# First FFN product of the first token block moved into the weight preparation of a gated-recurrence and FFN kernel

## Chip, cores and metric

The kernel runs on all 8 cores of one Trainium2 chip. Each core works on two of the 16 sequences and prepares all weights for itself. The metric is the device time in microseconds of the slowest core; a comparison takes the median of several runs.

## The reference, cut to what matters

```python
def attn(x, W_r, W_i, lambd):
    r = sigmoid(einsum('btd,ed->bte', x, W_r))
    i = sigmoid(einsum('btd,ed->bte', x, W_i))
    log_a = 8.0 * r * log_sigmoid(lambd)
    a = exp(log_a)
    b = sqrt(maximum(1.0 - exp(2.0 * log_a), 0.0)) * (i * x)
    return scan(h[t] = a[t] * h[t-1] + b[t])

def absmean(W):                       # ternary weights
    gamma = mean(abs(W)) + 1e-6
    return sign(W / gamma) * minimum(round(abs(W / gamma)), 1.0)

def ffn(x, W_fc, ln_w, ln_b, W_proj):
    h = gelu(einsum('btd,hd->bth', x, absmean(W_fc)))
    h = layernorm(h, ln_w, ln_b)
    return einsum('bth,dh->btd', h, absmean(W_proj))

x = x + attn(layernorm(x), W_r, W_i, lambd)
x = x + ffn(layernorm(x), W_fc, ln_w, ln_b, W_proj)
```

x is 16 sequences of 2048 tokens with D = 1024 channels, the hidden width H is 4096. Quantizing a weight needs the mean of its absolute values, so each weight is read twice: once for the sum, once to be compared with the threshold.

## The kernel before

A core takes its two sequences in eight blocks of T = 512 tokens (index k), channels on the partitions. A block's x is 8 tiles of 128 x 512 in `xb0` or `xb1`, by turns. For each k: layer norm 1 (`emit_ln1`), gates and scan (loop over e, lines 606 to 710), statistics of layer norm 2, its normalized tiles (`emit_ln2_tile_one`, six on VectorE and two on GpSimd), the first FFN product with Gelu (lines 761 to 792), and the second one (`emit_y_group`, spread over the gates of the next block). Block k = 0 also carries the preparation of the weights:

- Lines 210 to 226 convert W_r and W_i.
- During the gates of k = 0, `emit_gfc_loads` and `emit_gfc_abs` (L247, L257) read W_fc once and sum its absolute values.
- `emit_prep2a_mid` (lines 290 to 343) reads W_fc a second time in 32 pieces of 128 x 1024 (512 KB, L304) into four slots of `xb1`. VectorE quantizes each in two instructions (L319, L323) into `wfc_q`, which stays in SBUF. Beside it W_proj is read for the first time in 32 pieces (L314) into four slots made of the scratch tiles t_a, t_q, t_b, t_i, and ScalarE sums its absolute values (L331, activation Abs). After every second piece up to i = 14 one tile of layer norm 2 is emitted. The threshold of W_proj follows (`emit_thr`, L263).
- The FFN loop of k = 0 (lines 761 to 792): for each of 32 column blocks h, TensorE does 8 products (L767), ScalarE the Gelu (L775), GpSimd the square (L782; for k > 0 VectorE does it), and TensorE adds value and square into the statistics of layer norm 3, two blocks late (L753, L755, `emit_ln3_stat`). In the same loop W_proj is prepared piece by piece: `emit_prep2b_load` (L353) three pieces ahead, `emit_prep2b_piece` (VectorE L364 and L367, two small products L373 and L375), and `emit_prep2b_fold` two pieces late (VectorE L386, then a store to the DRAM buffer `wp_sc` by `emit_scatter`, L205).

The order of work is written by hand. Each engine runs its own list of instructions strictly in the order in which `emit` appended them, and a wait holds up all that stands behind it on that engine. DMAs are issued from such lists too: pieces in even slots from SyncE, those in odd slots from GpSimd. L304 and L314 of one slot count on one semaphore, and `emit` makes each DMA wait for the one before it on the same semaphore:

```python
            if inc.startswith("d_") and self.semc[inc] > 0:
                self.wait(eng, (inc, self.semc[inc]))
```

For an odd i GpSimd's list therefore has: wait until the slot is quantized (VectorE), issue L304, wait for its landing, issue L314.

Of the kernel before, what the change touches and what calls it, by code (L numbers as in the profile page):

```python
# [64 lines left out]
def build_nc(nsup=NSUP, debug=False):  # L65
# [221 lines left out]
        setfree(key, tln2)  # L287
        return tln2

    def emit_prep2a_mid(xb, tok_bc2, tok_i7, tok_gbl):  # L290
        nonlocal tok_wfc, tok_thrp
        ln2_toks = {}
        b.wait("tensor", gfc_state["last"])
        b.wait("tensor", tok_ones)
        tok_thrf = emit_thr(accf, 0, 0)
        red_p = None
        for i in range(32):
            pc, kd = i // 8, i % 8
# [26 lines left out]
            setfree(("qn4", sl), tq)
            setfree(("stg", sl), tq)
            if kd == 7:
                tok_wfc_pc[pc] = tq
            b.wait("scalar", tl2)
            red_p = b.emit("scalar", lambda E, st2=st2, i=i:  # L330
                           E.activation(st2, st2, AF.Abs, accum_out=accp[:, i:i + 1]), inc="s")  # L331
            setfree(("tstg", sl), red_p)
            if i % 2 == 0 and i // 2 < ND:
                ln2_toks[i // 2] = emit_ln2_tile_one(i // 2, xb, tok_bc2, tok_i7, tok_gbl)
        tok_wfc = tok_wfc_pc[3]
        b.wait("tensor", red_p)
        tok_thrp = emit_thr(accp, 1, 3)
        for sl in range(4):
            usewait("sync", ("stg", sl))
        dst1 = xping[1][:, :].rearrange("p (c t) -> p c t", c=ND)  # L340
        src1 = Xd[0, :, T:2 * T].rearrange("(c p) t -> p c t", p=128)
        tok_x[1] = b.emit("sync", lambda E, d=dst1, s=src1: E.dma_start(d, s), inc="d_x1", n=16)
        return (ln2_toks[5], ln2_toks[7])
# [252 lines left out]
    for k in range(nsup):  # L596
# [113 lines left out]
                emit_ln2_stat_chunk(k, xb, e - 1)  # L710

        tstat2 = emit_ln2_stat_chunk(k, xb, ND - 1)
        tok_bc2 = rows_and_bcast(tstat2, 2, rs_t, mb_t, prev_read=tok_ln1, prev_read_g=tok_ln1g)
        if k == 0:
            tok_ln2 = emit_prep2a_mid(xb, tok_bc2, tok_ri[(k, ND - 1)][1], tok_gb_last)
        else:
            lt = [emit_ln2_tile_one(c, xb, tok_bc2, tok_ri[(k, ND - 1)][1], tok_gb_last)
                  for c in range(ND)]
# [15 lines left out]
                src2 = Xd[sq2, :, t02:t02 + T].rearrange("(c p) t -> p c t", p=128)  # L734
                tok_x[kk] = b.emit("sync", lambda E, d=dst2, s=src2: E.dma_start(d, s), inc=f"d_x{kk % 2}", n=16)

        b.wait("tensor", tok_ln2[0])
        b.wait("tensor", tok_ln2[1])
        if k > 0:
            b.wait("tensor", tok_wfc)  # L740
        else:
            for i3 in range(3):
                emit_prep2b_load(i3)
        gs_toks = {}

        def emit_ln3_stat(h):
            tge2, tgs2 = gs_toks[h]
            b.wait("tensor", tge2)
            b.wait("tensor", tgs2)
            if h == 0:  # L750
                usewait("tensor", ("pS",))
                usewait("tensor", ("pQ",))
            b.emit("tensor", lambda E, h=h: E.matmul(pS[:, :], ones_bf[:, :], gch(h),  # L753
                                                     start=(h == 0), stop=(h == NH - 1)))
            tq = b.emit("tensor", lambda E, h=h: E.matmul(pQ[:, :], ones_bf[:, :],  # L755
                                                          gsq[:, (h % 3) * T:(h % 3 + 1) * T],
                                                          start=(h == 0), stop=(h == NH - 1)), inc="pe")
            setfree(("gsq", h % 3), tq)
            return tq

        for h in range(NH):
            bank = h % 4
            if k == 0:
                b.wait("tensor", tok_wfc_pc[h // 8])
            usewait("tensor", ("pool", bank))
            for d in range(ND):
                fn = lambda E, h=h, d=d, bank=bank: E.matmul(  # L767
                    pool[bank][:, :], wfc_q[:, d * H + h * 128: d * H + h * 128 + 128], lnch(d),
                    start=(d == 0), stop=(d == ND - 1))
                if d == ND - 1:  # L770
                    tu = b.emit("tensor", fn, inc="pe")
                else:
                    b.emit("tensor", fn)
            b.wait("scalar", tu)
            tge = b.emit("scalar", lambda E, h=h, bank=bank: E.activation(  # L775
                gch(h), pool[bank][:, :], AF.Gelu), inc="s")
            setfree(("pool", bank), tge)
            tok_gelu[(k, h)] = tge
            geng, ginc = ("gpsimd", "g") if k == 0 else ("vector", "v")
            b.wait(geng, tge)  # L780
            usewait(geng, ("gsq", h % 3))
            tgs = b.emit(geng, lambda E, h=h: E.tensor_tensor(  # L782
                gsq[:, (h % 3) * T:(h % 3 + 1) * T], gch(h), gch(h), ALU.mult), inc=ginc)
            gs_toks[h] = (tge, tgs)
            if k == 0:
                if h + 3 < NH:
                    emit_prep2b_load(h + 3)
                emit_prep2b_piece(h)
                if h >= 2:
                    emit_prep2b_fold(h - 2)  # L790
            if h >= 2:
                tq3 = emit_ln3_stat(h - 2)
        tq3 = emit_ln3_stat(NH - 2)
        tq3 = emit_ln3_stat(NH - 1)
        prev_rs3 = tok_yev.get((k - 1, ND - 1)) if k >= 1 else None
        if k == 0:
            emit_prep2b_tail()
# [96 lines left out]
```

How the kernel before makes its waits and increments, by code:

```python
    def emit(self, eng, fn, inc=None, n=1):  # L41
        if inc is not None:
            if inc.startswith("d_") and self.semc[inc] > 0:
                self.wait(eng, (inc, self.semc[inc]))
            self.semc[inc] += n
            tok = self.semc[inc]
            h = self.semh[inc]
            self.prog[eng].append(lambda E, fn=fn, h=h, n=n: fn(E).then_inc(h, n))
            return (inc, tok)
        self.prog[eng].append(fn)
        return None
# [1 line left out]
    def wait(self, eng, tok):  # L53
        if tok is None:
            return
        name, v = tok
        assert v <= self.semc[name], f"wait on future token {name}={v}"
        if self.maxw[eng].get(name, 0) >= v:
            return
        self.maxw[eng][name] = v
        h = self.semh[name]
        self.prog[eng].append(lambda E, h=h, v=v: E.wait_ge(h, v))
```

## Time and profile before

| | us |
|---|---|
| median of 3 runs (2371.64 to 2518.87) | 2372.93 |
| the profiled execution | 2364.18 |
| its span, slowest core | 2362.6 |
| spans of its eight cores | 2355.1 to 2362.6 |

The profiled execution is one run under the hardware profiler. The span goes from the first to the last instruction of a core; 1.6 us of the execution's time lie around it. The whole weight preparation lies in the first 502 us of it; the other seven token blocks take the rest. Engines are named PE (TensorE), DVE (VectorE), ACT (ScalarE), POOL (GpSimd) and SP (SyncE); PEld are the weight loads of TensorE. DMA-issuing instructions of GpSimd are listed with their engine but not counted as busy.

### The profile page before, as it was taken

To read this page: it belongs to the slowest core of one execution; us is meant where nothing else is said; L and a number is where in the kernel's file an instruction comes from. 1 tells how busy PE (TensorE), PEld (TensorE's weight loads), DVE (VectorE), ACT (ScalarE), POOL (GpSimd) and SP (SyncE) were. 2 spreads that over 40 slices of the span, in tenths; PEclk is the share of its full clock that TensorE was granted. 3 is DMA by queue.
4 is the path that set the end of the run, shared out by engine and by line. 5 is a ranking of instruction groups with operands and counts; after the bars stand their busy time and mean duration, and the time that the engine had idled before them with its cause. 6 is when DMAs were issued, how large, how long until landed. Compare 5 with 4: busy or idle time off the path is not lost.

```text
span 2362.6 us, 20089 instructions; the slowest of 8 cores (2355.1 to 2362.6 us)
## 1 busy us (share of the span) xinstructions
PE 1503.0 (64%) x6052; PEld 613.5 (26%) x6052; DVE 987.8 (42%) x1505; ACT 619.4 (26%) x1013; POOL 275.2 (12%) x260
## 2 busy tenths in 40 slices
PE   0333005755849685886769584958496767868597
PEld 0011001221314232332224131413142323323243
DVE  1423755645451444335442544244524443254413
ACT  0165221112322132223322232223221332223220
POOL 1211213421010101001010101010101001010100
PEclk9766557986969798888979796979798888979798
DMA  7564786751302130212121131123021212112103
GB/s 187 144 189 147 226 257 206 187 130 62 116 26 73 45 116 27 98 45 82 61 98 45 43 101 60 39 71 106 10 98 45 91 53 98 45 62 81 63 27 125
DMA packets 103746, 223.68 MB, mean 95 GB/s; under 512 B 34516, under 2 KB 34516, under 8 KB 103640
## 3 DMA queue, kind: packets, MB, share of 16 engines
q1 hardware_dynamic: 91352, 178.34, 23.6%
q0 software_dynamic: 12288, 44.05, 6.7%
q8 instruction: 52, 0.85, 0.1%
q14 instruction: 54, 0.44, 0.1%
HBM read 192.98 MB, written 29.37 MB: 94 GB/s over the span
## 4 chain that ended last, share of the span: by engine, by line
PE 44%; DVE 21%; ACT 12%; DMA 9%; issue 9%; POOL 3%; DVEq 1%; ACTq 0%; POOLq 0%; SPq 0%
PE pool L767 18%; PE pY L485 9%; PE pool L616 6%; DMA xb<-wfct 4%; DVE t_b L698 3%; POOL t_b L693 3%; PE pS L753 2%; PE pQ L755 2%; DVE tmp L586 2%; DVE ln_bf L588 2%; DVE tmp L284 2%; DVE ln_bf L286 2%; PE pS L459 2%; ACT t_a L657 2%; DVE t_q L682 2%
## 5 line engine op out<-in xcount | busy, mean ns | idle before, releaser
L767 PE MATMUL pool<-ln_bf,wfc_q 128*128 128x512 bf16 x2048 | 502.4, 391 | 99.6 <-DVE ln_bf L286 99.6
L485 PE MATMUL pY<-g_sb,wp_sl 128*128 128x512 bf16 x2048 | 472.6, 392 | 65.5 <-DVE tmp L507 47.3
L767 PEld LDWEIGHTS pool<-ln_bf,wfc_q 128*128 128x128 bf16 x2048 | 205.1, 101 | 367.7 <-issue 140.9
L485 PEld LDWEIGHTS pY<-g_sb,wp_sl 128*128 128x128 bf16 x2048 | 204.9, 100 | 326.7 <-issue 99.8
L775 ACT ACTIVATE g_sb<-pool 128x512 bf16<-128x512 f32 x256 | 152.9, 597 | 436.4 <-PE pool L767 436.3
L782 DVE TENSOR_TENSOR gsq<-g_sb 128x512 bf16<-128x512 bf16 x224 | 95.4, 426 | 389.3 <-ACT g_sb L775 377.0
L616 PE MATMUL pool<-ln_bf,wr_sl 128*128 128x512 bf16 x512 | 160.0, 469 | 114.3 <-DVE ln_bf L588 114.3
L651 ACT ACTIVATE t_r<-pool 128x512 f32<-128x512 f32 x64 | 38.1, 595 | 508.8 <-PE pool L616 508.8
L565 PE MATMUL pS<-xbr,ones_bf 128*128 128x512 bf16 x64 | 30.4, 475 | 211.6 <-DVE sqr L559 211.6
L693 POOL TENSOR_TENSOR t_b<-t_q,ln_bf 128x512 f32<-128x512 f32 x64 | 73.8, 1153 | 772.7 <-ACT t_q L687 772.7
L674 DVE SCALAR_TENSOR_TENSOR t_q<-t_a 128x512 f32<-128x512 f32 x64 | 44.3, 692 | 270.4 <-ACT t_a L662 270.4
L627 PE MATMUL pool<-ln_bf,wi_sl 128*128 128x512 bf16 x512 | 123.1, 384 | 0.0
L616 PEld LDWEIGHTS pool<-ln_bf,wr_sl 128*128 128x128 bf16 x512 | 59.6, 118 | 215.8 <-issue 180.3
L586 POOL TENSOR_TENSOR t_r<-xb,rs_t 128x512 f32<-128x512 f32 x16 | 25.6, 1598 | 759.7 <-DVE mb_t L469 758.5
L698 DVE TENSOR_TENSOR_SCAN t_b<-t_a,carry,t_b 128x512 f32<-128x512 f32 x48 | 61.6, 1284 | 104.8 <-POOL t_b L693 104.8
L753 PE MATMUL pS<-g_sb,ones_bf 128*128 128x512 bf16 x256 | 98.0, 383 | 4.0 <-DVE gsq L782 4.0
L755 PE MATMUL pQ<-gsq,ones_bf 128*128 128x512 bf16 x256 | 97.8, 382 | 0.0
L436 PE MATMUL pS<-xbr,ones_bf 128*128 128x512 bf16 x64 | 31.3, 490 | 103.8 <-DVE sqr L430 103.5
L459 PE MATMUL pS<-rows,ones_kf 1*128 1x512 f32 x48 | 41.6, 961 | 87.4 <-DVE rows L457 87.4
L446 ACT ACTIVATE rows<-pS,cst 1x512 f32<-1x512 f32 x24 | 16.3, 677 | 297.2 <-PE pQ L438 231.8
L263 PE MATMUL pool<-accp,ones_f 128*128 128x32 f32 x2 | 0.6, 396 | 127.2 <-ACT t_i L331 127.2
L682 DVE SCALAR_TENSOR_TENSOR t_q<-t_q,t_i 128x512 f32<-128x512 f32 x64 | 44.3, 692 | 64.5 <-ACT t_q L678 64.5
(118 smaller groups left out, 1667.0 us busy)
## 6 DMA issues: line engine op xcount, KB each, us to landing
wp_sl<-wp_sc SPq DMA_DIRECT2D x128, 512.0 KB, 3.9
xb<-x SPq DMA_DIRECT2D x8, 2048.0 KB, 9.6
wr_sl<-wr_sc SPq DMA_DIRECT2D x64, 256.0 KB, 3.1
wi_sl<-wi_sc SPq DMA_DIRECT2D x64, 256.0 KB, 2.9
xb<-wfct SPq DMA_DIRECT2D x32, 512.0 KB, 5.7
xb<-wfct POOLq DMA_DIRECT2D x32, 512.0 KB, 5.9
y<-xb SPq DMA_DIRECT2D x8, 2048.0 KB, 7.8
t_a<-wpt SPq DMA_DIRECT2D x16, 512.0 KB, 5.7
```

The lines of the kernel that those rows point to most:

```text
L459: tb1 = b.emit("tensor", lambda E: E.matmul(pS[:, :], ones_kf[:, :], s2, start=True, stop=True), inc="pe")
L485: fn = lambda E, kh=kh, sl=sl, bank=bank, first=(kh == 0), last=last: E.matmul(pY[bank][:, :], wp_sl[:, sl * 2048 + (kh % 16) * 128: sl * ...
L616: fn = lambda E, d=d, sl=sl, pR=pR: E.matmul(pR[:, :], wr_sl[:, sl * D + d * 128: sl * D + d * 128 + 128], lnch(d), start=(d == 0), stop=( ...
L627: fn = lambda E, d=d, sl=sl, pI=pI: E.matmul(pI[:, :], wi_sl[:, sl * D + d * 128: sl * D + d * 128 + 128], lnch(d), start=(d == 0), stop=( ...
L682: tvm = b.emit("vector", lambda E, q=q: E.scalar_tensor_tensor(t_q[:, q * T:(q + 1) * T], t_q[:, q * T:(q + 1) * T], 0.5, t_i[:, q * T:(q ...
L693: tgb = b.emit("gpsimd", lambda E, q=q, e=e: E.tensor_tensor(t_b[:, q * T:(q + 1) * T], t_q[:, q * T:(q + 1) * T], lnch(e), ALU.mult), inc ...
L698: tA = b.emit("vector", lambda E, q=q, init=init: E.tensor_tensor_scan(t_b[:, q * T:(q + 1) * T], t_a[:, q * T:(q + 1) * T], t_b[:, q * T: ...
L753: b.emit("tensor", lambda E, h=h: E.matmul(pS[:, :], ones_bf[:, :], gch(h), start=(h == 0), stop=(h == NH - 1)))
L755: tq = b.emit("tensor", lambda E, h=h: E.matmul(pQ[:, :], ones_bf[:, :], gsq[:, (h % 3) * T:(h % 3 + 1) * T], start=(h == 0), stop=(h == N ...
L767: fn = lambda E, h=h, d=d, bank=bank: E.matmul(pool[bank][:, :], wfc_q[:, d * H + h * 128: d * H + h * 128 + 128], lnch(d), start=(d == 0) ...
L775: tge = b.emit("scalar", lambda E, h=h, bank=bank: E.activation(gch(h), pool[bank][:, :], AF.Gelu), inc="s")
L782: tgs = b.emit(geng, lambda E, h=h: E.tensor_tensor(gsq[:, (h % 3) * T:(h % 3 + 1) * T], gch(h), gch(h), ALU.mult), inc=ginc)
```

## The change

24 of the 32 column blocks of the first FFN product of k = 0, with their Gelus, squares and statistics, move from the W_proj loop into the loop of `emit_prep2a_mid`: block i-8 is emitted at the end of iteration i, for i = 8 to 31. So that their input is there, the eight tiles of layer norm 2 are emitted in iterations 0 to 7, one each, where they were emitted in iterations 0, 2, ... 14. Blocks 24 to 31 stay in the W_proj loop, beside its first eight pieces, and its other 24 pieces have none beside them. For k > 0 nothing changes. The body of the FFN loop becomes the function `emit_ffn_h`; its square is on GpSimd for k = 0 as before. Lines move: the square is L758 after, the Gelu L751, the block's products L742.

```diff
@@ emit_prep2a_mid, end of the loop over i @@
-            if i % 2 == 0 and i // 2 < ND:
-                ln2_toks[i // 2] = emit_ln2_tile_one(i // 2, xb, tok_bc2, tok_i7, tok_gbl)
+            if i < ND:
+                ln2_toks[i] = emit_ln2_tile_one(i, xb, tok_bc2, tok_i7, tok_gbl)
+            if i >= 8:
+                emit_ffn_h(i - 8, ln2wait=(ln2_toks[5], ln2_toks[7]) if i == 8 else None)
@@ main loop, before the normalization of layer norm 2 @@
+        def emit_ffn_h(h, ln2wait=None):
+            bank = h % 4
+            if ln2wait is not None:
+                b.wait("tensor", ln2wait[0])
+                b.wait("tensor", ln2wait[1])
+            if k == 0:
+                b.wait("tensor", tok_wfc_pc[h // 8])
+            usewait("tensor", ("pool", bank))
...
+            b.wait("scalar", tu)
+            tge = b.emit("scalar", lambda E, h=h, bank=bank: E.activation(
+                gch(h), pool[bank][:, :], AF.Gelu), inc="s")
...
+            geng, ginc = ("gpsimd", "g") if k == 0 else ("vector", "v")
+            b.wait(geng, tge)
+            usewait(geng, ("gsq", h % 3))
+            tgs = b.emit(geng, lambda E, h=h: E.tensor_tensor(
+                gsq[:, (h % 3) * T:(h % 3 + 1) * T], gch(h), gch(h), ALU.mult), inc=ginc)
+            gs_toks[h] = (tge, tgs)
+            if h >= 2:
+                emit_ln3_stat(h - 2)
@@ main loop, in place of the loop over h @@
+            for j in range(8):
+                emit_ffn_h(24 + j)
+                emit_prep2b_load(j + 3)
+                emit_prep2b_piece(j)
+                if j >= 2:
+                    emit_prep2b_fold(j - 2)
+            for j in range(8, NH):
+                if j + 3 < NH:
+                    emit_prep2b_load(j + 3)
+                emit_prep2b_piece(j)
+                emit_prep2b_fold(j - 2)
```

GpSimd's list before, in the middle of `emit_prep2a_mid` (iterations 17, 19, 21 and 23): a load of W_fc into `xb`, a load of W_proj into t_q or t_i, and so on.

```order
L304 DMA xb<-wfct 128x1024 [waits v,d_stg1]
L314 DMA t_q<-wpt 128x1024 [waits s,d_stg1]
L304 DMA xb<-wfct 128x1024 [waits v,d_stg3]
L314 DMA t_i<-wpt 128x1024 [waits s,d_stg3]
L304 DMA xb<-wfct 128x1024 [waits v,d_stg1]
L314 DMA t_q<-wpt 128x1024 [waits s,d_stg1]
L304 DMA xb<-wfct 128x1024 [waits v,d_stg3]
L314 DMA t_i<-wpt 128x1024 [waits s,d_stg3]
```

The same place of GpSimd's list after the change:

```order
L304 DMA xb<-wfct 128x1024 [waits v,d_stg1]
L314 DMA t_q<-wpt 128x1024 [waits d_stg1]
L758 TENSOR_TENSOR gsq<-g_sb 128x512 [waits s,pe] x2
L304 DMA xb<-wfct 128x1024 [waits v,d_stg3]
L314 DMA t_i<-wpt 128x1024 [waits d_stg3]
L758 TENSOR_TENSOR gsq<-g_sb 128x512 [waits s,pe] x2
```

Two squares of `gsq`, each waiting for ScalarE (s) and TensorE (pe), now stand between the load of W_proj of one pair and the load of W_fc of the next.

ScalarE's list before, at the end of `emit_prep2a_mid` (the Abs of W_proj pieces, then all Gelus of k = 0):

```order
L331 ACTIVATE t_a,accp<-t_a 128x1024 [waits d_stg0]
L331 ACTIVATE t_q,accp<-t_q 128x1024 [waits d_stg1]
L331 ACTIVATE t_b,accp<-t_b 128x1024 [waits d_stg2]
L331 ACTIVATE t_i,accp<-t_i 128x1024 [waits d_stg3]
L775 ACTIVATE g_sb<-pool 128x512 [waits pe] x32
```

The same place after the change:

```order
L331 ACTIVATE t_a,accp<-t_a 128x1024 [waits d_stg0]
L751 ACTIVATE g_sb<-pool 128x512 [waits pe]
L331 ACTIVATE t_q,accp<-t_q 128x1024 [waits d_stg1]
L751 ACTIVATE g_sb<-pool 128x512 [waits pe]
L331 ACTIVATE t_b,accp<-t_b 128x1024 [waits d_stg2]
L751 ACTIVATE g_sb<-pool 128x512 [waits pe]
L331 ACTIVATE t_i,accp<-t_i 128x1024 [waits d_stg3]
L751 ACTIVATE g_sb<-pool 128x512 [waits pe] x9
```

A Gelu stands behind each Abs, and the last nine Gelus (blocks 23 to 31) follow the last Abs.

## Rows read from the trace of the kernel before

**Rows 1.** Busy time by stretches: start:end, length, engines, then PEclk, DMA share, GB/s

```profile
235.00:366.00 131.00, 3.78 (x9) 1.65 (x8) 77.84 (x82) 34.24 (x62) 22.85 (x34) 0.50 0.78 238
366.00:502.00 136.00, 99.31 (x385) 33.59 (x383) 90.62 (x102) 20.78 (x34) 61.55 (x62) 0.90 0.70 189
```

**Rows 2.** Waits from 235 to 366 us: us in total, times, longest

```profile
PE pool L263 <- ACT t_i L331: 127.2, 1, 127.2
```

**Rows 3.** Chain of waits from 220 to 580 us: start, us, what

```profile
289.59 7.86 DMA xb<-wfct
298.56 7.28 DMA xb<-wfct
```

**Rows 4.** Timeline of one pair: start, us, engine, line, tile, [idle before, releaser]

```profile
298.00 0.53 POOL L314 DMA_DIRECT2D t_i<-wpt  x1 [7.69 <-DMA xb<-wfct]
298.56 0.53 POOL L304 DMA_DIRECT2D xb<-wfct  x1
...
303.38 1.06 ACT L331 ACTIVATE t_i<-t_i 128x1024 f32<-128x1024 f32 x1 [8.59 <-DMA t_i<-wpt]
...
304.43 1.04 ACT L331 ACTIVATE t_a<-t_a 128x1024 f32<-128x1024 f32 x1
...
305.94 0.75 DVE L319 TENSOR_SCALAR qn_buf<-xb,thr 128x1024 bf16<-128x1024 f32 x1 [4.19 <-DMA xb<-wfct]
306.38 0.53 POOL L314 DMA_DIRECT2D t_q<-wpt  x1 [7.29 <-DMA xb<-wfct]
```

**Rows 5.** Timeline of GpSimd, first and last pair counted, and a layer norm tile

```profile
250.71 0.56 POOL L314 DMA_DIRECT2D t_q<-wpt  x1 [4.58 <-DVE wfc_q L323]
...
260.62 0.53 POOL L304 DMA_DIRECT2D xb<-wfct  x1
...
275.98 1.27 POOL L284 TENSOR_TENSOR t_r<-xb,rs_t 128x512 f32<-128x512 f32 x1
...
279.42 0.72 POOL L304 DMA_DIRECT2D xb<-wfct  x1
...
352.92 0.53 POOL L304 DMA_DIRECT2D xb<-wfct  x1
```

**Rows 6.** Timeline of TensorE, ScalarE and GpSimd: a block, table load, Gelu, square

```profile
365.92 3.19 PE L767 MATMUL pool<-ln_bf,wfc_q 128*128 128x512 bf16 x8
...
369.19 1.28 ACT L775 ACT_TABLE_LOAD   x1 [3.84 <-PE pool L767]
...
408.15 0.60 ACT L775 ACTIVATE g_sb<-pool 128x512 bf16<-128x512 f32 x1 [2.19 <-PE pool L767]
...
408.96 1.03 POOL L782 TENSOR_TENSOR gsq<-g_sb 128x512 bf16<-128x512 bf16 x1 [1.21 <-ACT g_sb L775]
```

**Rows 7.** The W_fc loads of L247, 82 to 198 us: issue to landing

```profile
DMA to landing us min/median/max: 4.0/5.2/7.8
```

**Rows 8.** Timeline of VectorE and GpSimd: piece 8, a steady pair, the end

```profile
402.13 0.82 DVE L364 TENSOR_SCALAR qn_buf<-t_a,thr 128x1024 bf16<-128x1024 f32 x1
...
469.17 1.26 DVE L386 TENSOR_SCALAR qn_buf<-qn_buf,lnw_pp 128x1024 bf16<-128x1024 bf16 x1
...
471.07 0.97 POOL L205 DMA_DIRECT2D wp_sc<-qn_buf  x1 [0.91 <-DVE qn_buf L386]
...
474.72 0.75 DVE L364 TENSOR_SCALAR qn_buf<-t_q,thr 128x1024 bf16<-128x1024 f32 x1 [1.83 <-DMA wp_sc<-qn_buf]
...
476.78 1.26 DVE L386 TENSOR_SCALAR qn_buf<-qn_buf,lnw_pp 128x1024 bf16<-128x1024 bf16 x1
...
501.26 0.67 DVE L404 COPY tmp<-pY 2x512 f32<-2x512 f32 x1
```

**Rows 9.** Waits of VectorE from 402 to 502 us

```profile
DVE qn_buf L364 <- DMA wp_sc<-qn_buf: 28.4, 12, 5.3
```

**Rows 10.** The folds of L386, 366 to 502 us: ns min/median/max

```profile
L386 DVE TENSOR_SCALAR qn_buf<-qn_buf,lnw_pp x32: 475/482/1265, 379.7 to 500.9; 128x1024 bf16<-128x1024 bf16 x32
```

**Rows 11.** Timeline of ScalarE: an Exp (L455) and the first Abs behind it

```profile
232.32 0.72 ACT L455 ACTIVATE rows<-rows,cst 1x512 f32<-1x512 f32 x1
232.95 1.04 ACT L331 ACTIVATE t_a<-t_a 128x1024 f32<-128x1024 f32 x1
```

More of the change, by code:

```diff
@@ L288, in emit_ln2_tile_one, with emit_prep2a_mid @@
         return tln2
-    def emit_prep2a_mid(xb, tok_bc2, tok_i7, tok_gbl):
+    def emit_prep2a_mid(xb, tok_bc2, tok_i7, tok_gbl, emit_ffn_h):
         nonlocal tok_wfc, tok_thrp
@@ L712, in build_nc, with emit_ln3_stat @@
         tstat2 = emit_ln2_stat_chunk(k, xb, ND - 1)
+        gs_toks = {}
+        ffn_state = {"tu": None}
+        def emit_ln3_stat(h):
+            tge2, tgs2 = gs_toks[h]
+            b.wait("tensor", tge2)
+            b.wait("tensor", tgs2)
+            if h == 0:
+                usewait("tensor", ("pS",))
+                usewait("tensor", ("pQ",))
+            b.emit("tensor", lambda E, h=h: E.matmul(pS[:, :], ones_bf[:, :], gch(h),
+                                                     start=(h == 0), stop=(h == NH - 1)))
+            tq = b.emit("tensor", lambda E, h=h: E.matmul(pQ[:, :], ones_bf[:, :],
+                                                          gsq[:, (h % 3) * T:(h % 3 + 1) * T],
+                                                          start=(h == 0), stop=(h == NH - 1)), inc="pe")
+            setfree(("gsq", h % 3), tq)
+            return tq
@@ new lines, in emit_ffn_h @@
+        def emit_ffn_h(h, ln2wait=None):
[6 more added lines that the diff above has]
+            usewait("tensor", ("pool", bank))
+            for d in range(ND):
+                fn = lambda E, h=h, d=d, bank=bank: E.matmul(
+                    pool[bank][:, :], wfc_q[:, d * H + h * 128: d * H + h * 128 + 128], lnch(d),
+                    start=(d == 0), stop=(d == ND - 1))
+                if d == ND - 1:
+                    tu = b.emit("tensor", fn, inc="pe")
+                else:
+                    b.emit("tensor", fn)
+            ffn_state["tu"] = tu
+            b.wait("scalar", tu)
+            tge = b.emit("scalar", lambda E, h=h, bank=bank: E.activation(
+                gch(h), pool[bank][:, :], AF.Gelu), inc="s")
+            setfree(("pool", bank), tge)
+            tok_gelu[(k, h)] = tge
+            geng, ginc = ("gpsimd", "g") if k == 0 else ("vector", "v")
[6 more added lines that the diff above has]
+                emit_ln3_stat(h - 2)
@@ L713, in build_nc @@
         tok_bc2 = rows_and_bcast(tstat2, 2, rs_t, mb_t, prev_read=tok_ln1, prev_read_g=tok_ln1g)
         if k == 0:
-            tok_ln2 = emit_prep2a_mid(xb, tok_bc2, tok_ri[(k, ND - 1)][1], tok_gb_last)
+            tok_ln2 = emit_prep2a_mid(xb, tok_bc2, tok_ri[(k, ND - 1)][1], tok_gb_last, emit_ffn_h)
         else:
@@ L735, in build_nc @@
                 tok_x[kk] = b.emit("sync", lambda E, d=dst2, s=src2: E.dma_start(d, s), inc=f"d_x{kk % 2}", n=16)
-        b.wait("tensor", tok_ln2[0])
-        b.wait("tensor", tok_ln2[1])
         if k > 0:
+            b.wait("tensor", tok_ln2[0])
+            b.wait("tensor", tok_ln2[1])
             b.wait("tensor", tok_wfc)
+            for h in range(NH):
+                emit_ffn_h(h)
         else:
@@ L743, in build_nc @@
                 emit_prep2b_load(i3)
[L744 to L792, printed above, removed]
@@ L793, in build_nc @@
+            for j in range(8):
[9 more added lines that the diff above has]
+                emit_prep2b_fold(j - 2)
         tq3 = emit_ln3_stat(NH - 2)
         tq3 = emit_ln3_stat(NH - 1)
+        tu = ffn_state["tu"]
```

## Prediction

> **What bounds the kernel now.** I read the busy time by stretches first, then the chain of waits, then the timeline of one pair of iterations, then the waits of the stage behind. The stretches [rows 1] split the preparation in two: 131 us in which TensorE is busy 3.78 us at the low level of its clock (granted 0.50, 1.2 of 2.4 GHz) while the DMA engines are busy 0.78 of the time (W_fc quantized, W_proj summed: call it stage A), and 136 us in which TensorE is busy 99 us at 0.90 (W_proj quantized, with the first FFN product beside it: stage B). In stage A the only large waiter is the threshold product of TensorE, 127.2 us for the last Abs [rows 2]. So TensorE has room for FFN work there, and the question is whether that work can be put in without slowing what paces the stage.
>
> What paces it is one queue. The chain of waits names the same piece again and again, a W_fc load issued by GpSimd [rows 3]. The timeline of one pair says why [rows 4]: L314 for an odd i is issued at 298.00, L304 for the next odd i right behind it at 298.56, and then GpSimd stands until that load has landed (ScalarE's Abs for the first starts at 303.38, VectorE takes the second at 305.94, GpSimd goes on at 306.38). The two loads of a slot share a semaphore, and each issue waits for the one before on it, so the queue has two loads in flight and turns once per landing. From the L304 of i=9 at 260.62 to that of i=31 at 352.92 are 11 pairs [rows 5]: 92.3 us, 8.39 each.
>
> **The change, part by part.** (1) 24 of the 32 FFN column blocks move into stage A, one per iteration from i=8. On TensorE that is free: a block took 3.27 us there at the low level (365.92 to the table load that waited for it at 369.19) [rows 6]; the two statistics products of a block, as wide as one of its eight each, are then a quarter of that, 0.8. Two blocks with theirs are 8.2 us per pair, below the period that follows. On ScalarE two Gelus of 0.60 us per pair are small too.
>
> (2) The squares L782 (L758 after) are on GpSimd, and there they stand between the DMA issues. After the change GpSimd's row per pair is L304, L314, square, square. The first square waits for Gelu(i-8), and on ScalarE that stands behind Abs(i), which waits for the L314 load that GpSimd has just issued. The second stands behind Abs(i+1) and Gelu(i-7). Only then comes the next L304. Nothing of this queue is in flight meanwhile; SyncE runs ahead but VectorE takes the slots in order and so is paced by GpSimd too. The new period is the sum of what lies in series:
> - L304 issued until its data are in: T. The trace has 7.38 us (298.56 to 305.94), but behind another load of the same queue; L314, which is first in its queue, has 5.38 (298.00 to 303.38) with three more loads in flight [rows 4]. The shortest landing of a W_fc load in the earlier stage is 4.0 us [rows 7]. After the change each load is alone in its queue, with about one of SyncE beside it; I take the middle of 4.0 and 5.4: 4.7.
> - GpSimd goes on 0.44 us after VectorE does (305.94, 306.38) [rows 4]: 0.45.
> - L314 until Abs(i): T again, 4.7.
> - Abs(i) to Gelu(i-8) 1.05 (303.38 to 304.43 is Abs to the next on ScalarE [rows 4]), Gelu 0.60, Abs(i+1) 1.05, Gelu start to square start 0.81 and the square 1.03 (408.15, 408.96) [rows 6]: 4.54. Its data are there, since SyncE is ahead.
> Sum 9.4 + 0.45 + 4.54 = 14.4 us in place of 8.39. Over 11 pairs: 158.4 against 92.3, +66.1. With T = 4.0 for both it is 13.0 and +50.6; with today's 7.38 and 5.38, 17.8 and +103.
>
> (3) The second layer norm's tiles are all in the first eight iterations. VectorE's have no price of their own: GpSimd's path is later. GpSimd's two tiles go from i=12 and 14 to 6 and 7, 3.44 us each (275.98 to the next issue at 279.42) [rows 5]. From L314 of i=5 at 250.71: tile 6 until 254.7, L304 of i=7, which lands about 261 (6 us, since SyncE's queue is full here), L314 at 261.5, tile 7 until 265.5, then FFN block 0, 3.3 (268.8), table load 1.3, Gelu to square 0.81 and square 1.03: about 272.2 for the L304 of i=9, before at 260.62 [rows 5, 6]. +11.6.
>
> (4) What follows the last load is as before: the 2 MB load of x and the first W_proj loads start off VectorE's last quantization. 0.
>
> (5) Stage B. Its first eight pieces still have a block each (24 to 31): nothing. The other 24 took from 402.13 to 501.26, 99.1 us or 8.26 per pair [rows 8]. VectorE is short of nothing but the store of two pieces ahead: it waited 28.4 us, 12 times, each for a store to wp_sc [rows 9], and all of them for GpSimd's. The steady pair: fold ends 470.43, store issued 471.07, buffer free 474.72 (4.29), piece 2.06, fold 1.26 [rows 8] = 7.6. The fold takes 0.482 at the median and 1.265 at the longest [rows 10], the long ones beside work on GpSimd. With no square beside it, I count 0.48: 0.78 by 12 pairs = 9.4 gained; if the rest above 7.6 (0.66 a pair) goes as well, 17. I take -13. Bounds: 0, if stores and loads are the limit; -38, if VectorE alone sets the pace (24 by 2.54 = 61).
>
> For the fold the Trainium skill (SBUF — State Buffer, section SBUF: two separate sides) has a rule: VectorE in a two-port mode and GpSimd share one port pair, the second to come waits for the whole instruction, and descriptors that GpSimd writes for its own DMAs wait too. The long folds agree with it. By the rule alone every long fold goes with the squares, which is the -9.4, and GpSimd's store issue, which stays, may keep some; the sum is the same within that.
>
> Sum: 66.1 + 11.6 - 13 = +64.7 on the profiled execution's 2364.2 us: 2428.9. The median of the runs shown is 2372.9, 8.7 above it, so 2438 for the median after.
>
> **Rivals.**
> - The work fits in the gaps (other side). If the squares stall GpSimd only while it would have waited for its load anyway, stage A keeps 8.39 per pair and only stage B changes: -13, at best -38, so 2335 to 2360. For it: GpSimd stands idle 6 to 8 us of each pair today. Against: that idle time is the landing of a load in flight, and the new waits come when none is. The point from which it decides: with the 11.6 us of the start and -13 behind, nothing is lost up to 8.5 us a pair, and with the whole -38 up to 10.8; the series has 5.0 us before any load, so both landings together would have to take under 3.5 or under 5.8. 0.06.
> - Loads quicken and stage B gains much. T = 4.0 and -30: 50.6 + 11.6 - 30 = +32, 2405, within 2%. For it: stage A moved 238 GB/s [rows 1] and would move some 150; stage B has 28 us of waits to lose. 0.15.
> - Loads stay as slow as now, T of 5.4 for both: 15.8 per pair, +81 + 12 - 10 = +83, 2456. It is inside my case.
> - Table loads. Abs and Gelu now alternate on ScalarE. If each switch loads a table as at 369.19 (1.28 us) [rows 6], four more per pair lie on the series: 5.1 by 11 = 56 more, 2494. Against: Abs follows Exp at 232.95 with no load between [rows 11], so Abs needs none of its own there. 0.06.
>
> The Trainium skill (ScalarE: Activation LUTs, section Table sets: the hidden batching unit) says to batch calls by table set, which speaks against alternating; but it also says that cheap functions, abs among them, are in every set. By its first sentence this rival's time, by the second none of it. The rows above bear the second out for the Exp set; for Gelu's no row here does, hence 0.06.
>
> **How the numbers follow.** My case, series of waits with T of 4.0 to 5.4 and a stage B gain of 5 to 20, gives +45 to +92 and gets 0.73; the rivals 0.06, 0.15 and 0.06. A measurement tells about 2% from no change, 47 us here, so my case is over it save for its lowest edge (0.05). Slower 0.68 + 0.06 = 0.74. Same 0.05 + 0.15 + 0.06 = 0.26, of which 0.02 goes to faster, for both stages beating their bounds: 0.24 and 0.02. Range: 2400 (the second rival's figure, a little below) to 2468 (T of 5.4 with a small gain in stage B); the table case and a full fit are left out.
>
> **What would show it.** Right: GpSimd's L304 issues in stage A some 14 us apart; its squares waiting for Gelu; ScalarE's Abs on GpSimd's loads waiting 8 us or more, those on SyncE's none; DMA share in stage A down from 0.78 to 0.45 or 0.5; threshold product of W_proj near 443; the last 24 pieces of stage B at about 7.2 a pair; one table load for the Gelus. Wrong: a period of 10 us or less, table loads between Abs and Gelu, or stage B shorter by over 25 us.

## The result, and the profile after

| | before | after |
|---|---|---|
| median of the runs, us | 2372.41 (10 runs) | 2433.15 (9 runs) |
| profiled execution, us | 2364.18 | 2429.75 |
| its span, slowest core, us | 2362.6 | 2427.9 |

The ratio of the changed kernel to the one before is 1.0253, 95% interval [1.0239, 1.0267]: slower by 61 us. In some executions of any kernel the cores of one die run at a lower granted clock and the time is some per cent longer: the medians given here include such executions and the ratios leave them out (without them e7, below, has 2354 in place of 2361, e9 2357 in place of 2359), and e4 is read from cores 0 to 3, which were undisturbed.

First the busy time by stretches of the changed kernel (start:end, length, PE, PEld, DVE, ACT, POOL, then TensorE's clock, DMA share, GB/s): stage A, and the 11 pairs inside it alone. GpSimd's DMA issues do count as busy in such rows, otherwise than said ahead: of its 45 instructions in the second row 23 are squares and 22 are issues.

```profile
235.00:435.00 200.00, 77.34 (x238) 28.39 (x242) 77.00 (x82) 46.26 (x85) 45.14 (x56) 0.67 0.49 155
274.00:423.00 149.00, 67.73 (x217) 24.95 (x219) 43.85 (x44) 34.70 (x66) 34.55 (x45) 0.73 0.45 147
```

Against [rows 1] TensorE has found its work in stage A, but the DMA share has fallen from 0.78 to 0.49, and the rate from 238 to 155 GB/s. Nothing more had to be loaded; the loads are only further apart.

One pair of the changed kernel on its timeline (start, length, engine, line, tile, idle before and releaser), the counterpart of [rows 4]:

```profile
302.86 0.59 POOL L304 DMA_DIRECT2D xb<-wfct  x1
...
307.56 0.75 DVE L319 TENSOR_SCALAR qn_buf<-xb,thr 128x1024 bf16<-128x1024 f32 x1 [9.10 <-DMA xb<-wfct]
308.01 0.53 POOL L314 DMA_DIRECT2D t_q<-wpt  x1 [4.56 <-DMA xb<-wfct]
...
311.93 1.06 ACT L331 ACTIVATE t_q<-t_q 128x1024 f32<-128x1024 f32 x1 [10.25 <-DMA t_q<-wpt]
...
312.98 0.58 ACT L751 ACTIVATE g_sb<-pool 128x512 bf16<-128x512 f32 x1
...
313.46 1.04 ACT L331 ACTIVATE t_b<-t_b 128x1024 f32<-128x1024 f32 x1
313.77 1.03 POOL L758 TENSOR_TENSOR gsq<-g_sb 128x512 bf16<-128x512 bf16 x1 [5.23 <-ACT g_sb L751]
314.50 0.58 ACT L751 ACTIVATE g_sb<-pool 128x512 bf16<-128x512 f32 x1
...
315.29 1.04 POOL L758 TENSOR_TENSOR gsq<-g_sb 128x512 bf16<-128x512 bf16 x1 [0.48 <-ACT g_sb L751]
...
316.27 0.59 POOL L304 DMA_DIRECT2D xb<-wfct  x1
```

GpSimd's part of it reads from top to bottom as one series. GpSimd issues a load, waits 4.56 us for it, issues the second, and waits 5.23 us for a Gelu that stands behind the Abs of that second load. Before, the second row of [rows 4] (the next L304) came 0.56 us after L314; now it comes 8.3 us after it. No ACT_TABLE_LOAD stands between Abs and Gelu; the one load is here, ahead of the first Gelu:

```profile
271.60 1.28 ACT L751 ACT_TABLE_LOAD   x1 [2.81 <-PE pool L742]
```

The table gives each kernel of this study by the same marks: the start of GpSimd's L304 of i=9, the mean distance of its L304s from i=9 to i=31, the first quantization of stage B, the time of its first 8 pieces, and of its last 24. Each figure is the median over the cores of one profiled execution, read from each core's timeline.

| kernel | L304 of i=9 | pair | stage B starts | first 8 pieces | last 24 pieces | median, us |
|---|---|---|---|---|---|---|
| before | 258.9 | 8.28 | 369.5 | 29.2 | 99.6 | 2372 |
| after | 273.7 | 13.57 | 442.7 | 30.7 | 88.0 | 2433 |
| e1 squares on VectorE | 262.1 | 7.35 | 365.2 | 29.8 | 88.1 | 2353 |
| e2 squares behind the issue | 263.0 | 8.19 | 374.2 | 30.4 | 88.4 | 2361 |
| e3 tiles only | 262.7 | 7.69 | 367.7 | 29.9 | 100.6 | 2369 |
| e4 wait only | 266.3 | 12.72 | 427.2 | 29.3 | 99.4 | 2429 |
| e5 before, squares on VectorE | 258.5 | 8.25 | 370.7 | 65.8 | 195.9 | 2502 |
| e6 own semaphores | 263.3 | 6.67 | 359.2 | 30.1 | 88.3 | 2345 |
| e7 tiles behind the issue | 260.9 | 7.39 | 365.7 | 30.4 | 88.5 | 2361 |
| e8 contiguous store | 263.8 | 7.27 | 366.3 | 28.5 | 83.1 | 2344 |
| e9 square behind the piece | 259.5 | 8.16 | 370.5 | 27.1 | 88.9 | 2359 |
| e10 as e6, tiles moved | 262.3 | 6.64 | 358.1 | 30.0 | 89.3 | 2344 |
| e11 no block moved | 255.8 | 6.67 | 354.1 | 27.3 | 90.0 | 2339 |
| e12 late squares | 261.9 | 6.68 | 358.2 | 27.5 | 86.0 | 2339 |

For the change itself the first two rows say: +14.8 us up to the L304 of i=9, +58.2 in the 11 pairs (5.29 each), about nothing around stage B's start, +1.5 in its first 8 pieces and -11.6 in the rest.

### The profile page after: what moved, and what is told of

Same layout as the page of the kernel before. It is cut to its first block, busy times and chain, and to the rows that moved or that the text cites. A ratio compares the mean times of both kernels' runs of the same rounds, so it can differ in the third digit from the quotient of the medians.

```text
span 2427.9 us, 19960 instructions; the slowest of 8 cores (2412.8 to 2427.9 us)
## 1 busy us (share of the span) xinstructions
PE 1523.6 (63%) x5932; PEld 619.0 (25%) x6052; DVE 978.7 (40%) x1505; ACT 616.7 (25%) x1013; POOL 271.2 (11%) x260
## 4 chain that ended last, share of the span: by engine, by line
PE 42%; DVE 21%; ACT 13%; issue 10%; DMA 10%; POOL 3%; DVEq 1%; ACTq 0%; POOLq 0%; SPq 0%
PE pool L742 17%; PE pY L487 9%; PE pool L618 6%; DVE t_b L700 3%; POOL t_b L695 3%; DMA xb<-wfct 3%; DMA wp_sc<-qn_buf 3%; PE pQ L727 2%; DVE tmp L588 2%; DVE ln_bf L590 2%; PE pS L725 2%; DVE tmp L284 2%; DVE ln_bf L286 2%; PE pS L461 2%; ACT t_a L659 2%
## 5 line engine op out<-in xcount | busy, mean ns | idle before, releaser
L742 PE MATMUL pool<-ln_bf,wfc_q 128*128 128x512 bf16 x2005 | 514.0, 400 | 146.7 <-DVE ln_bf L286 99.4
L742 PEld LDWEIGHTS pool<-ln_bf,wfc_q 128*128 128x128 bf16 x2048 | 208.0, 102 | 426.6 <-issue 209.9
L758 DVE TENSOR_TENSOR gsq<-g_sb 128x512 bf16<-128x512 bf16 x224 | 95.3, 426 | 389.1 <-ACT g_sb L751 376.9
L751 ACT ACTIVATE g_sb<-pool 128x512 bf16<-128x512 f32 x256 | 152.5, 596 | 362.3 <-PE pool L742 360.0
L319 DVE TENSOR_SCALAR qn_buf<-xb,thr 128x1024 bf16<-128x1024 f32 x32 | 25.0, 781 | 111.8 <-DMA xb<-wfct 111.6
```

What stands on the lines that cost most here:

```text
L742: fn = lambda E, h=h, d=d, bank=bank: E.matmul(pool[bank][:, :], wfc_q[:, d * H + h * 128: d * H + h * 128 + 128], lnch(d), start=(d == 0) ...
L758: tgs = b.emit(geng, lambda E, h=h: E.tensor_tensor(gsq[:, (h % 3) * T:(h % 3 + 1) * T], gch(h), gch(h), ALU.mult), inc=ginc)
```

## The experiments

Each ratio is to executions of the kernel before that were timed together with that experiment. Diffs are cut to the lines that matter; a `...` marks a cut.

**e1, the squares of the moved blocks on VectorE.** GpSimd's list in stage A has only its loads left; TensorE and ScalarE still do the moved blocks.

```diff
-            geng, ginc = ("gpsimd", "g") if k == 0 else ("vector", "v")
+            geng, ginc = ("gpsimd", "g") if k == 0 and h >= 24 else ("vector", "v")
```

> The changed kernel with the squares of blocks 0 to 23 on VectorE, so that GpSimd's list in stage A holds only its loads again. Theory (the squares' waits in GpSimd's list hold up the next load): the period from one L304 of GpSimd to the next over one falls from 13.5 us to 8.4 to 9.0 us, and the time from 2433 to about 2380 (2372 to 2390). Rival (the FFN work itself slows stage A, by sharing SBUF, the DMA engines' memory or ScalarE): the period stays over 12 us and the time over 2420.

Measured: 2353.25 us, ratio 0.9934 [0.9917, 0.9951]; a pair takes 7.35 us. Against the changed kernel that is 80 us less for one line, and it is faster than the kernel before by 0.7%, where 2372 to 2390 had been expected. The expectation missed two things: the pair is shorter than before, of which e3 shows a part (7.69, since no tile stands between the pairs any more), and stage B keeps its gain of 11.5 us. The moved work as such doesn't slow stage A, and the rival falls.

**e2, the squares on GpSimd, but where it waits anyway.** They stand behind the issue of L304 and ahead of L314, where GpSimd waits for its first load.

```diff
+            if i % 2 == 1 and i >= 11:
+                emit_sq(i - 11)
+                emit_sq(i - 10)
...
```

The squares leave `emit_ffn_h` for blocks 0 to 23, and the statistics products follow two blocks later than in the changed kernel.

> The changed kernel with the same squares on the same engine, but two iterations later, between the issues of L304 and L314 of an odd i, where GpSimd waits for a landing anyway; the statistics products follow two blocks later. Theory (the wait at that place, not the work, costs): the period is 8.4 to 9.2 us, GpSimd waits for no Gelu, the time is 2370 to 2385. Rival (the 2.1 us of squares per pair count in full): the period is 10.5 us or more and the time 2395 or more.

Measured: 2361.02 us, ratio 0.9964 [0.9951, 0.9978], 8.19 us a pair, both a little better than expected (2370 to 2385, 8.4 to 9.2). GpSimd's timeline of one pair, with VectorE's quantization of the piece that L304 loads (L314 and L319 are L317 and L322 in this kernel):

```profile
299.22 0.53 POOL L304 DMA_DIRECT2D xb<-wfct  x1
299.76 1.46 POOL L741 TENSOR_TENSOR gsq<-g_sb 128x512 bf16<-128x512 bf16 x1
...
306.64 0.75 DVE L322 TENSOR_SCALAR qn_buf<-xb,thr 128x1024 bf16<-128x1024 f32 x1 [3.48 <-DMA xb<-wfct]
...
307.21 1.08 POOL L741 TENSOR_TENSOR gsq<-g_sb 128x512 bf16<-128x512 bf16 x1 [5.99 <-ACT g_sb L763]
308.24 0.59 POOL L317 DMA_DIRECT2D t_q<-wpt  x1
308.83 0.53 POOL L304 DMA_DIRECT2D xb<-wfct  x1
```

Same engine, same work, 5.4 us less per pair than the changed kernel: the work of the squares was not what cost. The expectation that GpSimd would find every Gelu done was wrong (it waits 5.99 us for the second), but a load of its own is in flight meanwhile. That load is there at 306.64, so only the last 1.2 us or so of wait and square are not covered (306.64 and the 0.44 of GpSimd's delay, to 308.24). Over the pairs it is 8.19 us against e1's 7.35, where GpSimd has no square at all.

**e3, the layer norm tiles alone.** The kernel before, with the change's condition for the tiles and nothing else.

```diff
-            if i % 2 == 0 and i // 2 < ND:
-                ln2_toks[i // 2] = emit_ln2_tile_one(i // 2, xb, tok_bc2, tok_i7, tok_gbl)
+            if i < ND:
+                ln2_toks[i] = emit_ln2_tile_one(i, xb, tok_bc2, tok_i7, tok_gbl)
```

> The kernel before with the eight tiles of layer norm 2 in iterations 0 to 7, no FFN block moved. Theory (of the 14.0 us that the changed kernel loses ahead of the L304 of i=9 the two tiles on GpSimd are a part, the wait for FFN block 0 and its Gelu the rest): that L304 comes 3 to 7 us later than before, and the time rises by 0 to 5 us, since the tiles no longer stand between later loads. Rival (VectorE's six tiles in a row set the start): 10 us or more later.

Measured: 2368.52 us, ratio 0.9994 [0.9976, 1.0011]; the L304 of i=9 comes 3.8 us later, and the pairs behind it take 7.69 us, since the tiles stand between none of them. So 3.8 of the 14.8 us are the tiles. The other 11 are the wait for block 0 and its square: e1 has the tiles and the block but not that wait, and its L304 of i=9 comes at 262.1, as here.

**e4, the wait alone.** The kernel before with one wait more per iteration on GpSimd. No work is added, removed or moved.

```diff
             setfree(("tstg", sl), red_p)
+            if i >= 8:
+                b.wait("gpsimd", red_p)
```

> The kernel before with one wait added per iteration from i=8: GpSimd waits for that iteration's Abs on ScalarE before its next load. Nothing is computed more, less or elsewhere. Theory (a wait behind the landing of L314 puts both landings in series): the period rises from 8.39 to 11.6 us (13.5 less two Gelus of 0.48 and a square of 1.0), over 11 pairs +35 us, time 2400 to 2415. Rival (waiting in GpSimd's list fits in the time in which it waits for landings anyway): the period stays under 9 us and the time within 5 us of before.

Measured: 2429.32 us, ratio 1.0244 [1.0222, 1.0266]. The wait alone costs 58 of the change's 61 us, though the change also gains 11.6 in stage B that this kernel doesn't: in stage A it costs 57.7 us where the change costs 73.2 (stage B starts at 427.2 and 442.7, before at 369.5). It is more than the 30 to 45 expected. The waits of core 2 in the last seven pairs (323 to 406 us; us in total, times, longest):

```profile
POOL xb L304 <- ACT t_a L331: 24.4, 4, 6.3
POOL t_q L314 <- DMA xb<-wfct: 18.4, 4, 5.0
POOL xb L304 <- ACT t_b L331: 18.3, 3, 6.2
POOL t_i L314 <- DMA xb<-wfct: 14.5, 3, 5.0
```

Seven waits of 6.1 us for an Abs and seven of 4.7 for a landing: both landings in series. The L304s of these seven pairs are 11.9 us apart (322.99 to 406.11), close to the 11.6 expected. What the expectation left out are the two tiles at i=12 and 14, which lie in the open in this kernel, and the first wait, which delays the L304 of i=9 by 7.4 us.

**e5, a control that became a finding.** The kernel before with all squares of the first block on VectorE.

```diff
-            geng, ginc = ("gpsimd", "g") if k == 0 else ("vector", "v")
+            geng, ginc = ("vector", "v")
```

> The kernel before with all squares of the first token block on VectorE and no FFN block moved: the control for e1, which was 17 us faster than before. Theory (e1 gains because 24 pieces of stage B have no FFN block and no GpSimd square beside them, and pays nothing in stage A): VectorE gets 0.43 us of square per piece and saves about as much on its folds, so this kernel stays within 5 us of before (2366 to 2376). Rival (e1 gains merely by freeing GpSimd of the squares): about 2353 too.

Measured: 2502.39 us, ratio 1.0559 [1.0528, 1.0589], neither of the two. Stage B takes 262 us in place of 129. VectorE's timeline there:

```profile
423.02 0.42 DVE L782 TENSOR_TENSOR gsq<-g_sb 128x512 bf16<-128x512 bf16 x1 [5.16 <-ACT g_sb L775]
423.36 0.75 DVE L364 TENSOR_SCALAR qn_buf<-t_b,thr 128x1024 bf16<-128x1024 f32 x1
...
430.67 0.43 DVE L782 TENSOR_TENSOR gsq<-g_sb 128x512 bf16<-128x512 bf16 x1 [4.78 <-ACT g_sb L775]
```

The view shows one engine; the rest is read from the lists. The square of block h stands in front of piece h and waits 5 us for its Gelu; on TensorE block h+1 stands behind the products of piece h. So VectorE, TensorE and ScalarE take turns, 7.65 us from one square to the next here.

**e6, more loads in flight.** e1 with semaphores `d_tst0` to `d_tst3` for the W_proj loads, in both stages.

```diff
-                         E.dma_start(st2, WPT[128 * i:128 * (i + 1), :]), inc=f"d_stg{sl}", n=16)
+                         E.dma_start(st2, WPT[128 * i:128 * (i + 1), :]), inc=f"d_tst{sl}", n=16)
...
```

> e1 with semaphores of their own for the W_proj loads, so that L314 no longer waits for the landing of L304 of its slot: up to eight loads are in flight in stage A where there were four. Theory (the period is the landing time that stands in GpSimd's list): GpSimd's period falls from 7.9 us to 7.0 or less and the time from 2353 to 2343 or less. Rival (four loads in flight already take all the bandwidth that the eight cores share, some 265 GB/s each): landings get longer instead, the period stays at 7.6 to 8.0 and the time within 4 us of e1.

Measured: 2345.05 us, ratio 0.9892 [0.9858, 0.9926], 6.67 us a pair. The stretch of its stage A (same columns as above), then the landings there (count, KB each, median us):

```profile
265.00:335.00 70.00, 49.46 (x187) 19.97 (x192) 48.05 (x61) 31.58 (x58) 12.72 (x22) 0.82 0.97 299
```

```profile
xb<-wfct POOLq DMA_DIRECT2D x11, 512.0 KB, 9.0
t_i<-wpt POOLq DMA_DIRECT2D x5, 512.0 KB, 11.6
```

A landing takes 9 to 12 us and still the pair is shorter: with more in flight GpSimd no longer waits for the landing, but ahead of L304, where its list asks for the slot that VectorE frees. From 265 to 335 us five of these waits, 25.8 us, end with VectorE's L323, five more, 27.0 us, the profile puts down to ScalarE, and none to a landing. A DMA share of 0.97 leaves little for still more loads in flight; no run tried them.

**e7, GpSimd's tiles behind the issue.** e1 with the two tiles between L304 and L314 of iterations 5 and 7.

```diff
+            if i in (5, 7):
+                c = 6 + (i - 5) // 2
+                ln2_toks[c] = emit_ln2_tile_one(c, xb, tok_bc2, tok_i7, tok_gbl)
...
-            if i < ND:
+            if i < 6:
```

> e1 with GpSimd's two tiles of layer norm 2 placed between the issues of L304 and L314 of iterations 5 and 7, where it waits for a landing. Theory (a tile in front of an L304 delays it by its 3.4 us, behind it by nothing): the L304 of i=9 comes 2 to 6 us earlier than in e1, and the time falls by 2 to 5 us, to about 2350. Rival (the start is paced by VectorE's quantization, which does not change): the same as e1 within 2 us.

Measured: 2360.74 us, ratio 0.9937 [0.9912, 0.9961], beside e1's 0.9934. The L304 of i=9 came 1.2 us earlier, not 2 to 6: a miss, and the time is the rival's. In place of its tiles GpSimd now waits for VectorE's list ahead of L304: 1.9 to 3.2 us for that of i=7 and 0.3 to 3.2 us for that of i=9, on every core (releaser VectorE L284).

**e8, the store as contiguous rows.** e1 with the pieces stored as rows of 2048 bytes, for the cost of the 256-byte runs of the stores in stage B. It leaves out the right layout: the second product reads its weights in a wrong order.

```diff
-        dst = wp_sc[:, :, i * 128:(i + 1) * 128].transpose([1, 0, 2])
-        src2 = qh.rearrange("p (kd j) -> p kd j", kd=ND)
+        dst = wp_sc.rearrange("k p (q j) -> (k p q) j", j=1024)[128 * i:128 * (i + 1), :]
+        src2 = qh
```

> e1 with every piece of W_proj stored as rows of 2048 bytes in a permuted layout of the same buffer, in place of runs of 256 bytes; the second FFN product then reads its weights in a wrong order (left out: the right layout). Same bytes, an eighth of the packets. Theory (without FFN blocks the pieces of stage B are paced by the cycle fold, store, free buffer, and the 256-byte packets make the store long): stores land in 2.5 to 3 us, VectorE's waits for them mostly go, the last 24 pieces fall from 88 us to 65 to 75, the time to about 2335. Rival (the loads of W_proj, or the memory that all cores share, set the pace): the last 24 pieces stay over 82 us.

Measured: 2343.81 us, two runs, ratio 0.9890 [0.9861, 0.9918]. The store issues of the last 24 pieces (count, KB each, median us to landing), of e1 from 403 to 490 us:

```profile
wp_sc<-qn_buf POOLq DMA_DIRECT2D x12, 256.0 KB, 3.7
...
wp_sc<-qn_buf SPq DMA_DIRECT2D x12, 256.0 KB, 4.0
```

and of e8 from 398 to 482 us:

```profile
wp_sc<-qn_buf SPq DMA_DIRECT2D x13, 256.0 KB, 3.7
wp_sc<-qn_buf POOLq DMA_DIRECT2D x13, 256.0 KB, 2.7
```

The landings are shorter by 0.3 us on one queue and 1.0 on the other, but the pieces take 83.1 us, 5 less than e1, far from 65 to 75 and on the rival's side (over 82). The DMA share falls from 0.76 to 0.67 in these windows. So the 256-byte runs are a small part of stage B; what holds the rest was not separated. The time falls by 9 us against e1, of which about 6 show in stage B; where the rest lies is open.

**e9, e5 with the square one piece later.**

```diff
...
                 emit_prep2b_piece(h)
+                if h >= 1:
+                    emit_sq(h - 1)
+                if h == NH - 1:
+                    emit_sq(h)
```

> e5 (the kernel before with the first block's squares on VectorE, no FFN block moved; it took 2502 us) with each square one piece later in VectorE's list: the square of block h-1 stands behind piece h instead of the square of block h in front of it. Theory (in e5 VectorE waits for Gelu h before piece h, while TensorE's block h+1 stands behind the products of piece h, so the engines work in series, some 8 us per piece where there were 4.2): with the square behind the piece VectorE finds Gelu h-1 done, the 24 last pieces fall from 196 us to 95 to 105 and the time to 2360 to 2385. Rival (VectorE has too little time for squares in stage B): it stays over 2420.

Measured: 2359.19 us, ratio 0.9941 [0.9920, 0.9962]. 143 us come back by the place of one instruction in VectorE's list, slightly more than expected (2360 to 2385; 95 to 105 for the last 24 pieces). More important for the change: the last 24 pieces take 88.9 us with their FFN blocks beside them, and 88.0 in the changed kernel without. The folds there (ns min/median/max):

```profile
L386 DVE TENSOR_SCALAR qn_buf<-qn_buf,lnw_pp x26: 477/479/614, 416.1 to 501.9; 128x1024 bf16<-128x1024 bf16 x26
```

Against [rows 10] the long folds are gone; GpSimd computes nothing here, its 31 instructions from 370 to 502 us are all DMA issues. What stage B gained in the changed kernel can be had by taking the squares off GpSimd, with every FFN block left in place. Whether the short folds or GpSimd's freer list of stores bring it, no run takes apart.

**e10, e6 with both tiles of GpSimd behind its two issues of iteration 7.**

```diff
+            if i == 7:
+                for c in (6, 7):
+                    ln2_toks[c] = emit_ln2_tile_one(c, xb, tok_bc2, tok_i7, tok_gbl)
...
-            if i < ND:
+            if i < 6:
```

> The fastest version so far (e6: squares of blocks 0 to 23 on VectorE, semaphores of their own for the W_proj loads) with GpSimd's two tiles of layer norm 2 both behind the two issues of iteration 7. Theory (in e6 stage A is paced by the DMA engines, 0.95 busy and 314 GB/s, so an issue that comes 3.4 us earlier is served no sooner): within 3 us of e6's 2345, ratio to before 0.987 to 0.991. Rival (the start still waits for GpSimd's issue of iteration 7): 3 to 5 us less than e6.

Measured: 2343.60 us, ratio 0.9899 [0.9865, 0.9933]: as e6.

**e11, no block moved.** e9 with e6's semaphores; the loop of stage A is that of the kernel before.

```diff
-                         E.dma_start(st2, WPT[128 * i:128 * (i + 1), :]), inc=f"d_stg{sl}", n=16)
+                         E.dma_start(st2, WPT[128 * i:128 * (i + 1), :]), inc=f"d_tst{sl}", n=16)
...
                 emit_prep2b_piece(h)
+                if h >= 1:
+                    emit_sq(h - 1)
...
```

> e9 (no FFN block moved, tiles where they were, squares on VectorE behind the piece) with semaphores of their own for the W_proj loads. It asks what moving 24 blocks is worth when nothing stands in GpSimd's list: e6 has both with the blocks moved, 2345. Theory (e9's last 24 pieces take 89 us with the blocks beside them and e1's 88 without, so the blocks cost nothing in stage B and moving them gains nothing): 2343 to 2353. Rival (moving them is worth the 6 us between e1 and e9): 2350 to 2356 or more.

Measured: 2338.57 us, ratio 0.9863 [0.9840, 0.9885], better than either expectation and the fastest with e12.

**e12, all blocks' squares off GpSimd, with the blocks moved.** e6 with the squares of blocks 24 to 31 on VectorE, one piece late.

```diff
             for j in range(8):
                 emit_ffn_h(24 + j)
                 emit_prep2b_load(j + 3)
                 emit_prep2b_piece(j)
+                if j >= 1:
+                    emit_sq(23 + j)
...
+                emit_ln3_stat(22 + j)
+            emit_sq(31)
```

> e6 (blocks moved, own semaphores) with the squares of blocks 24 to 31 on VectorE too, one piece late as in e9, so GpSimd does no square at all. Theory (beside the squares on GpSimd the folds are long and its stores late): the first eight pieces fall from 30 us to 27 to 29 as in e9, the time to about 2343. Rival (in the first eight pieces TensorE's low clock and the landing of x set the pace): no change from e6's 2345 within 2 us.

Measured: 2338.85 us, ratio 0.9868 [0.9848, 0.9889]. The first eight pieces take 27.5 us in place of e6's 30.1, as expected, and the time falls by somewhat more than expected. With the blocks moved 2338.85, without 2338.57: once no list holds up the loads, no worth of moving the 24 blocks can be seen, within the 0.2% of the intervals. The table shows two parts that cancel. With the blocks moved stage B starts 4.1 us later (358.2 against 354.1, since the L304 of i=9 comes 6.2 us later), and its last 24 pieces take 4.0 us less (86.0 against 90.0). So the blocks do cost stage B something, but no more than moving them costs stage A; what holds the start, the tiles or the block, was not separated here.

## Why the prediction was right

It forecast 2438 (2400 to 2468), slower; the result is 2433. Its steps against the rows:

- **What paces stage A** (GpSimd's list, one landing per pair). Right. e1 and e2 take the wait out of that list, each in another way, and the loss goes; e4 puts the wait alone into the kernel before and has 58 us of loss.
- **The period, 14.4 us.** Measured 13.54 on the shown core (core 6; 274.62 to 423.55), 13.57 at the median. Its terms in the pair above: the first landing 4.70 (4.7 said), GpSimd's delay 0.45 (0.45), the second landing 3.92 (4.7), Abs to next issue 4.34 (4.54). Over the 88 pairs of all cores the medians are 4.88, 0.45, 3.83 and 4.34, which add up to 13.5. The term that was mis-sized is the second landing: it is shorter than the middle of 4.0 and 5.4, and shorter than the first by a microsecond, where the prediction took one T for both. The bounds, 13.0 and 17.8, held. Over 11 pairs +56.6 on that core, where +66.1 was said.
- **The start, +11.6.** Measured +14.0 on the shown cores, +14.8 at the median. The step that failed is "VectorE's have no price of their own: GpSimd's path is later". Block 0 began at 267.95, when VectorE had quantized piece 7, and not at 265.5 behind GpSimd's tile, which was done at 263.81. The rows there:

```profile
261.08 1.61 DVE L286 TENSOR_TENSOR ln_bf<-tmp,mb_t 128x512 bf16<-128x512 f32 x1
262.28 1.53 POOL L286 TENSOR_TENSOR ln_bf<-t_r,mb_t 128x512 bf16<-128x512 f32 x1
262.62 1.75 DVE L319 TENSOR_SCALAR qn_buf<-xb,thr 128x1024 bf16<-128x1024 f32 x1
...
265.67 0.75 DVE L319 TENSOR_SCALAR qn_buf<-xb,thr 128x1024 bf16<-128x1024 f32 x1
266.52 1.28 DVE L323 SCALAR_TENSOR_TENSOR wfc_q<-xb,thr,qn_buf 128x1024 bf16<-128x1024 f32 x1
...
267.95 7.38 PE L742 MATMUL pool<-ln_bf,wfc_q 128*128 128x512 bf16 x21 [30.02 <-DVE wfc_q L323]
```

  L286 and L319 took 1.61 and 1.75 us while GpSimd worked on its tile, in place of 0.69 and 0.75; that is 1.9 us on VectorE's path. The prediction's own terms add up to 271.9 for this L304, not 272.2, so +11.3.
- **Stage B, -13.** At the median over the cores -11.6 in the last 24 pieces and +1.5 in the first 8. The shown core is a poor one: 474.68 to 567.25 is 92.6 us, where the median core has 88.0, so the profile page of one core would have given -6.6. The reason given, GpSimd's squares beside the folds and its stores, is borne out by e9; no FFN block had to leave for it.
- **TensorE in stage A "at the low level".** Not so throughout: its granted clock is 0.73 over the pairs, where it had been 0.50 with TensorE idle. It changed nothing: TensorE is busy 67.7 of the 149 us, and even the 8.2 us a pair that the prediction took at the low level lie below 13.5.
- **The errors cancel in part.** The period was said 9.5 us too dear over the pairs, the start 2.4 too cheap and stage B, on that core, 6.4 too generous; ahead of stage B's first piece 1.5 us went missing and its first 8 pieces took 3.4 more, both said to be 0. That the sum, +64.7, is so near the +65.6 of the two profiled executions is therefore luck in part. The medians differ by 60.7, since the 8.7 us between profile and median did not carry over: after, the profiled execution lies 3.4 us below the median.
- **The range.** "+45 to +92" doesn't follow from its own terms: T of 4.0 with a gain of 20 is 50.6 + 11.6 - 20 = +42, T of 5.4 with a gain of 5 is 81 + 12 - 5 = +88, so 2461 at the top and not 2468. The measurement lies well inside either.
- **The rivals.** "The work fits in the gaps" falls by the period of 13.57 and by e4. "Loads quicken and stage B gains much": the loads did come down to 4.70 and 3.92, but stage B's last 24 pieces gained 11.6 at the median and not 30. Table loads: one for all Gelus. Here the second sentence that was cited from the Trainium skill (ScalarE: Activation LUTs, section Table sets: the hidden batching unit) holds for Gelu's table too, with 24 alternations and no load between. For the folds, the rule of the Trainium skill (SBUF — State Buffer, section SBUF: two separate sides) agrees with the longest fold of 614 ns in e9, where GpSimd computes nothing, against 1265 before.

## What to carry to other kernels

An engine that issues DMAs carries more in its list than its own work: before moving an instruction onto it, or into the place between two issues, follow what the instruction waits for. If that is data which the same engine has just requested, two landings come into series, and the wait costs up to a landing per turn, while the squares' own 2.1 us a pair cost under 1 where a load was in flight (e4: 58 us for no work at all; e2 against e1: 8.19 and 7.35 us a pair). On an engine that issues no DMA the place counts as much: one square further back in VectorE's list gave 143 us (e5, e9). And an idle engine beside a busy DMA queue is no reason to move work there: ask first whether the stage that the work leaves was waiting for it. Here it was to a small part (4 us, e12 against e11), and moving it cost as much ahead; the gain of stage B was to be had by taking the squares off GpSimd (e9, e11).

## What the runs showed of the hardware

- With one semaphore for two loads of 512 KB, and the wait that `emit` puts between them, at most four were in flight: 258 GB/s and a DMA share of 0.83 from 260 to 353 us of the kernel before. With semaphores of their own (e11) the same loads ran at 307 GB/s and 0.97 from 260 to 330 us, with all eight cores loading, though a landing took 10.3 to 12.8 us at the medians of its buffers there, where it had taken 5.0 to 6.5.

```profile
260.00:353.00 93.00, 0.00 (x0) 0.00 (x0) 51.66 (x50) 25.55 (x46) 19.20 (x28) 0.50 0.83 258
```

```profile
260.00:330.00 70.00, 0.00 (x0) 0.00 (x0) 46.65 (x46) 21.73 (x38) 16.81 (x24) 0.50 0.97 307
```

- GpSimd goes on 0.44 us after VectorE when both wait for the same landing (305.94 and 306.38 before, 307.56 and 308.01 after): 0.45 us in all 88 pairs of the changed kernel's eight cores.
- A store of 256 KB in runs of 256 bytes landed in 3.7 to 4.0 us at the median (e1), the same bytes in rows of 2048 in 2.7 to 3.7 (e8), beside the same loads: runs of an eighth of the length cost less than a factor of two here.
